# Zeroing the masked keys of three narrow-head attention blocks on GpSimd instead of masking their key-major scores on TensorE

## The chip, the cores and the metric

One core of one Trainium2 chip runs the whole program in one launch. The metric is the device time of that core in microseconds (us), the median of several runs. TensorE multiplies, VectorE (DVE in the rows) and ScalarE (ACT) work elementwise and can read PSUM, GpSimd (POOL) works elementwise on SBUF, SyncE (SP) issues loads and stores.

## What is computed

A decoder of two layers over 4 sequences of 256 tokens and width 256, all in float32. Each line is a residual step with a layer norm behind it:

```python
x = layernorm(x + L0_attn(x))            # a: 16 heads of 128, window of 64
x = layernorm(x + L0_xattn(x, ctx))      # b: 16 heads of 16, causal, first 256 rows of ctx
x = layernorm(x + L0_ffn(x))             # c: 8 experts, 2 per token
x = layernorm(x + L1_attn(x))            # d: 32 heads of 8, 8 key heads, causal
x = layernorm(x + L1_xattn(x, ctx))      # e: latent attention over 1601 keys
x = layernorm(x + L1_ffn(x))             # f: 16 heads of 16, causal; g: 8 experts, 2 per token
```

The three blocks b, d and f all compute

```python
scores = einsum('bqhd,bkhd->bhqk', q, k) * scale
scores = where(key <= query, scores, -inf)
out = einsum('bhqk,bkhd->bqhd', softmax(scores), v)
```

## The kernel before

The letters a to g name the stages, which run one after the other; `narrow_attention` (line 830) builds b, d and f. Its **unit** is four heads of one sequence; `n` counts them, 16 in b and f (`U` = 4 per sequence), 32 in d (`U` = 8). A score matrix of 256 x 256 has three blocks of 128 x 128 that matter (`TILES_OF`): two on the diagonal, numbers 0 and 2, and one under it.

The scores are computed twice. Query-major scores (a query per partition) lie in PSUM banks 0 to 2 (`A_BANK`) and serve only for the row maxima: four reductions on VectorE (`maxima`, lines 1314 to 1317). The negated maxima are transposed by TensorE (`turn_maxima`, line 1064) and added to the queries (`lower_queries`, line 1324) in spare lanes of the contraction, so that the key-major scores (a key per partition, banks 3 to 5, `B_BANK`) come out with the maximum subtracted. ScalarE takes their exponential in one instruction of 1536 columns into `PT` (`exponentials`, line 1236; the tile is called landing in b and f, d_PT in d). `values` (line 1118) multiplies `PT` with the values and with ones; VectorE inverts the sums and multiplies (`normalise`, lines 1330 and 1334).

The causal mask is a matrix product too. `mask_queries` and `mask_keys` (lines 1074, 1078) each multiply the bf16 mask by the identity into the eight diagonal blocks of a bank group, ahead of the scores that are added onto it. In the rows `mask_keys` is `ident_b,mask_b` and `mask_queries` is `mask_b,ident_b`; all of these go through the helper on line 100.

TensorE's order is written out by hand in the loop of line 1143. Iteration `i` does: `mask_queries` for unit i+2 (waits for the maxima of unit i+1), the scores of both forms (query-major for i+2, key-major for i, woven together, with `lowered` of i waited for), `turn_maxima` of i+1, `values` of i-1, a wait for the exponential of i, `mask_keys` for i+1, and then what lies beside (`beside`, line 908): projections for the next sequence, the output projection, a transposition of the next norm, in d also steps of stage e (class `Latent`). A projection in the bank `SIDE` first waits for `lowered` of i+1. VectorE does the maxima of i+2, `lower_queries` of i+1, then `normalise`, norms and additions. `PT` has two buffers: the exponential of n waits for `values` of n-2.

GpSimd has little to do in these blocks: it clears buffers, in b and f makes three tables for the router (`gate_gpsimd`, line 1480) and at the end scatters rows (`scatter`, line 1603), and in d ropes the context of stage e (`rope_context`, line 2191, four instructions for each of 4 sequences), makes its low part (`lower_kv`, line 2209, after ScalarE's `upper_kv`, line 2107) and starts on the first queries (`rope_q`, `lower_z`). `gpsimd_early` (line 2231) lists these in one run. ScalarE makes the copies of `upper_kv` in the iterations that `KEPT_BESIDE` names, and SyncE loads the context of sequences 2 and 3 when roping of sequences 0 and 1 is done (line 2032).

Of the kernel before, what the change touches and what calls it, by code (L numbers as in the profile page):

```python
# [16 lines left out]
P = 128  # L17
# [37 lines left out]
def decoder(nc, t, out):  # L55
    with ExitStack() as top:
# [773 lines left out]
        def narrow_attention(name, block, hd, heads, kv_heads, lane, before, following, carried=(3,), entering=(),  # L830
# [13 lines left out]
            with ExitStack() as sc:  # L844
# [48 lines left out]
                scored1, exped, valued = signal("scored1"), signal("exped"), signal("valued")  # L893
                inverted, o_made, summed, added = signal("inverted"), signal("o_made"), signal("summed"), signal("added")

# [76 lines left out]
                def tensor():  # L972
# [94 lines left out]
                    def masked(k):  # L1067

                        for block in (0, 2):
                            for j in range(4):  # L1070
                                at, col = place(block, j)
                                yield bank[k + at][:, col * P:(col + 1) * P], block == 0 and j < 3

                    def mask_queries():
                        for o, first in masked(A_BANK):
                            mm(o, ident_b[:], causal, first, False)
# [41 lines left out]
                    def values(n):  # L1118
# [4 lines left out]
                        pe.wait_ge(*exped.at(n + 1))  # L1123
# [19 lines left out]
                    for i in range(FIRST, LAST + 1):  # L1143
# [261 lines left out]
                def gpsimd():  # L1405
                    pool.wait_ge(*before)
# [554 lines left out]
        class Latent:  # L1961
# [3 lines left out]
            KEPT_BESIDE = {3: 0, 4: 1, 7: 2, 10: 3}  # L1965
# [225 lines left out]
            def rope_context(self, b):  # L2191
                landed, x, r, k = landings["e"], self.ctx_raw[b % 2], self.swapped[b % 2], self.roped[b % 2]
                cosines, sines = self.ropek[:, 0, :, :], self.ropek[:, 1, :, :]
                if b == 0:
# [578 lines left out]
```

## Time and profile before

| | |
|---|---|
| median of 3 runs | 2019.15 us (2017.1 to 2019.63) |
| the profiled execution | 2011.26 us, its span 2009.9 us |
| mean granted TensorE clock | 0.965 |
| TensorE, VectorE, ScalarE, GpSimd busy | 1847.1, 1291.5, 1083.5, 603.4 us |
| stage b / d / f, roughly | 290 to 420 / 598 to 830 / 1695 to 1827 us of the span |

A row of a timeline gives the start in us from the start of the span, the duration, the engine, the line of the kernel, the operation, what it writes and reads with shapes, how many instructions are merged, and in brackets how long the engine stood idle before it and what ended that. PE is TensorE's matrix product and PEld its weight load. TensorE's instructions are pipelined, so a row's duration reaches beyond the start of the next one: of two successive groups the distance of their starts tells what one costs. PEclk is the share of TensorE's full clock (2.4 GHz) that was granted; 0.50 is the low level, 1.2 GHz. The chain that ended last goes back from the last instruction, at each step to what released it.

### The profile page before, as it was taken

The page shows a single profiled execution, that of the slowest core. Times are in us where ns is not written, and L with a number is a line of the kernel's source. Part 1 is how long each engine was busy: PE and PEld are TensorE (multiplying, and loading weights), DVE is VectorE, ACT ScalarE, POOL GpSimd, SP SyncE. Part 2 cuts the span into 40 slices and gives each one's busy share as a digit, 9 for nine tenths or more (in the row PEclk, how much of TensorE's full clock was granted, in tenths as well). Part 3 has the DMA queues.
Part 4 walks back from the last instruction along what each step waited for, and adds up shares of the span by engine and source line. Part 5 has one row for each costly group of instructions (what it writes and reads, how often), then busy time and mean ns, then how long its engine had stood idle before and what let it go on. Part 6 is the DMA issues. An engine that isn't in the chain of part 4 may idle for free.

```text
span 2009.9 us, 42825 instructions
## 1 busy us (share of the span) xinstructions
PE 1847.1 (92%) x16214; PEld 1539.6 (77%) x16214; DVE 1291.5 (64%) x3373; ACT 1083.5 (54%) x2729; POOL 603.4 (30%) x543
## 2 busy tenths in 40 slices
PE   7989988979998999789999999999999997897995
PEld 6988976646656767589999999999999985774663
DVE  5576655752236555468888888888888887775222
ACT  5756653312213333468878888888888873331221
POOL 5633320032223200334444443334444430003221
PEclk9999999979998999889999999999999998997998
DMA  4000009222238000000000000000000002402223
GB/s 158 12 1 1 1 26 365 81 89 39 47 57 258 2 2 2 21 11 11 12 12 11 27 12 11 11 11 12 12 11 1 1 1 88 175 3 78 40 46 66
DMA packets 51864, 91.75 MB, mean 46 GB/s; under 512 B 4592, under 2 KB 43632, under 8 KB 49232
## 3 DMA queue, kind: packets, MB, share of 16 engines
q1 hardware_dynamic: 42784, 77.64, 11.6%
q0 software_dynamic: 8160, 10.29, 3.3%
q8 instruction: 134, 2.20, 0.4%
q10 hardware_dynamic: 720, 1.09, 0.2%
q14 instruction: 66, 0.54, 0.1%
HBM read 56.13 MB, written 32.87 MB: 44 GB/s over the span
## 4 chain that ended last, share of the span: by engine, by line
PE 72%; DVE 16%; issue 4%; ACT 3%; POOL 2%; DMA 2%; SPq 0%; ACTq 0%; DVEq 0%; POOLq 0%
PE bank L100 60%; PE bank L2355 9%; DVE e_st L2508 1%; DVE e_PT_lo L2527 1%; DVE a_t L640 1%; DVE d_nm L1315 1%; PE bank L1729 1%; POOL g_rows L1609 1%; POOL c_rows L1609 1%; PE bank L440 1%; PE bank L193 1%; DVE f_nm L1315 1%; DVE d_nm L1314 1%; DVE tiny L125 1%; DVE b_nm L1315 1%
## 5 line engine op out<-in xcount | busy, mean ns | idle before, releaser
L2508 DVE TENSOR_REDUCE e_st<-bank 128x1 f32<-128x401 f32 x512 | 291.2, 569 | 143.2 <-PE bank L100 135.7
L2445 ACT ACTIVATE e_P<-bank,e_st 128x400 f32<-128x400 f32 (+1 forms) x512 | 307.5, 601 | 104.6 <-DVE e_st L2512 103.8
L2527 DVE TENSOR_TENSOR e_PT_lo<-bank,e_PT_hi 128x512 fp32r<-128x512 f32 (+1 forms) x448 | 287.7, 642 | 0.0
L2355 PE MATMUL bank<-ident,e_P 128*128 128x128 f32 (+1 forms) x1664 | 260.4, 276 | 16.8 <-DVE e_PT_lo L2527 6.7
L2460 ACT CAST e_PT_hi<-bank 128x512 fp32r<-128x512 f32 (+1 forms) x448 | 248.3, 554 | 26.3 <-PE bank L2355 11.8
L100 PE MATMUL bank<-e_PT_hi,e_kv 128*128 128x256 f32 (+1 forms) x832 | 250.6, 321 | 0.0
L2355 PEld LDWEIGHTS bank<-ident,e_P 128*128 128x128 f32 (+1 forms) x1664 | 196.5, 141 | 53.2 <-issue 37.8
L100 PE MATMUL bank<-e_PT_lo,e_kv 128*128 128x256 f32 (+1 forms) x832 | 217.2, 281 | 0.0
L100 PE MATMUL bank<-e_KT,e_qk_hi 128*128 128x402 f32 x512 | 195.0, 381 | 9.7 <-ACT e_P L2445 6.5
L100 PE MATMUL bank<-e_KT,e_qk_lo 128*128 128x402 f32 x512 | 177.5, 347 | 0.0
L100 PEld LDWEIGHTS bank<-e_PT_lo,e_kv 128*128 128x128 f32 (+1 forms) x832 | 159.6, 192 | 0.0
L100 PEld LDWEIGHTS bank<-e_PT_hi,e_kv 128*128 128x128 f32 (+1 forms) x832 | 158.9, 191 | 0.1
L2219 POOL TENSOR_TENSOR x_in<-x_in,e_ropeq 96x512 f32<-96x512 f32 x32 | 41.2, 1287 | 343.7 <-ACT x_in L2144 343.7
L100 PE MATMUL bank<-mask_b,ident_b 128*128 128x128 bf16 (+1 forms) x878 | 123.6, 270 | 13.0 <-DVE XT_lo L206 7.1
L100 PEld LDWEIGHTS bank<-e_KT,e_qk_hi 128*128 128x128 f32 x512 | 96.4, 188 | 27.2 <-ACT e_P L2445 23.1
L2219 POOL TENSOR_TENSOR e_r<-x_in,e_ropeq 96x512 f32<-96x512 f32 x32 | 41.0, 1283 | 226.5 <-ACT x_in L2144 226.5
L100 PEld LDWEIGHTS bank<-mask_b,ident_b 128*128 128x128 bf16 x878 | 68.5, 101 | 47.9 <-issue 19.0
L2445 ACT ACTIVATION_READ_ACCUMULATOR e_P<-bank,e_st 128x1 f32 x512 | 102.6, 200 | 0.0
L100 PEld LDWEIGHTS bank<-e_KT,e_qk_lo 128*128 128x128 f32 x512 | 97.2, 190 | 0.0
L1236 ACT ACTIVATE d_PT<-bank 128x1536 f32<-128x1536 f32 x32 | 46.5, 1452 | 89.0 <-PE bank L100 89.0
L1236 ACT ACTIVATE landing<-bank 128x1536 f32<-128x1536 f32 x32 | 46.4, 1451 | 81.9 <-PE bank L100 81.9
L100 PE MATMUL bank<-g_wall,g_xT 128*128 x184 | 88.0, 602 | 0.8 <-ACT g_xT L1783 0.8
(448 smaller groups left out, 4935.8 us busy)
## 6 DMA issues: line engine op xcount, KB each, us to landing
c_wall<-in_c_w SPq DMA_DIRECT2D x8, 1536.0 KB, 19.2
g_wall<-in_g_w SPq DMA_DIRECT2D x8, 1536.0 KB, 19.5
c_rows<-normed SPq DMA_DIRECT2D x9, 1040.0 KB, 12.0
g_rows<-normed SPq DMA_DIRECT2D x9, 1040.0 KB, 12.9
e_stage<-in_e_w SPq DMA_DIRECT2D x16, 416.0 KB, 3.2
c_xs<-c_rows SPq DMA_DIRECT2D x23, 130.0 KB, 2.1
g_xs<-g_rows SPq DMA_DIRECT2D x23, 130.0 KB, 2.1
landing<-in_a_wo SPq DMA_DIRECT2D x2, 1024.0 KB, 6.1
```

Source lines behind the costliest of these rows:

```text
L100: return pe.matmul(o, a, b, start=start, stop=stop, skip_group_check=True)
L125: dve.tensor_tensor(s, s, v, ALU.mult).then_inc(link.sem, 1)
L193: last = pe.transpose(view[:, c, i * P:(i + 1) * P], src[:, i, c * P:(c + 1) * P], ident[:])
L1236: act.activation(PT[n % 2].rearrange("p a j n -> p (a j n)"), psum[:, B_BANK:B_BANK + 3, :].rearrange("p a n -> p (a n)"), ACT.Exp, scale= ...
L1315: dve.tensor_reduce(out1[:, 0:3], a[:, :, P:3 * P], AX.X, ALU.max, negate=True)
L1609: pool.indirect_dma_start(scratch[self.name][0][:, :], bass.IndirectOffsetOnAxis(ap=self.slots[:, n, k:k + 1], axis=0), self.payload[:, n, ...
L2219: pool.tensor_tensor(x1, v, self.ropeq[:, 0:2, :], ALU.mult)
L2355: last = pe.transpose(o[0:rows, c * SEQ + i * P:c * SEQ + (i + 1) * P], p[:, i, k0:k0 + rows], ident[:])
L2445: act.activation(Pm[u % 2][:, i, j * PIECE:j * PIECE + n], bank[score_bank[j]][:, 0:n], ACT.Exp, bias=s[:, i, 4:5], accum_out=s[:, i, j:j ...
L2460: act.copy(PT[at % PT_BUFS][0][0:rows, 0:n, :], bank[tb_bank[at % 2]][0:rows, 0:n * SEQ].rearrange("p (c n) -> p c n", c=n)).then_inc(*pt_ ...
L2508: last = dve.tensor_reduce(s[:, i, j:j + 1], bank[score_bank[j]][:, 0:PIECE + 1], AX.X, ALU.max)
L2527: dve.tensor_tensor(lo, bank[tb_bank[at % 2]][0:rows, 0:n * SEQ].rearrange("p (c n) -> p c n", c=n), hi.bitcast(F32), ALU.subtract).then_i ...
```

## The change

`mask_keys` goes. The key-major scores are computed without the mask; the first product into each of their three banks (head j = 3) now carries the start flag, and the wait for the exponential of the unit before (or, for the first unit, for `v_kept`) stands in `scores` instead of ahead of `mask_keys`. GpSimd then zeroes the exponentials of keys behind their query: `select(n)` waits for the exponential of n and runs two `affine_select` in place on `PT`, over six and two blocks of 128 x 128, and `values(n)` waits for `selected` instead of `exped`. `mask_queries` stays.

Since `select(n)` is wanted in each unit, GpSimd's other work is spread: the router's tables come after the select of unit 1, and in d `rope_context` is cut into three parts that follow the selects of units 0 to 11, with `lower_kv` after those of units 3, 4, 8 and 12. ScalarE's `upper_kv` of sequences 2 and 3 moves from iterations 7 and 10 to 8 and 12.

```diff
-                    def mask_keys():
-                        for o, first in masked(B_BANK):
-                            mm(o, causal, ident_b[:], first, False)
...
-                        return mm(o, k if keys_first else q, q if keys_first else k, False, True)
+                        return mm(o, k if keys_first else q, q if keys_first else k, keys_first and j == 3, True)
...
                         if n1 is not None:
                             pe.wait_ge(*lowered.at(n1 + 1))
+                            if n1 == 0:
+                                pe.wait_ge(*v_kept.at(1))
+                            else:
+                                pe.wait_ge(*exped.at(n1))
...
-                        pe.wait_ge(*exped.at(n + 1))
+                        pe.wait_ge(*selected.at(n + 1))
...
-                        if 0 <= i + 1 < N:
-                            if i >= 0:
-                                pe.wait_ge(*exped.at(i + 1))
-                            else:
-                                pe.wait_ge(*v_kept.at(1))
-                            mask_keys()
...
+                    def select(n):
+
+                        p = PT[n % 2]
+                        pool.wait_ge(*exped.at(n + 1))
+                        for blocks, pattern in ((p[:, :, 0:3:2, :], [[0, 3], [0, 2], [1, P]]), (p[:, 0:3:2, 3, :], [[0, 2], [1, P]])):
+                            last = pool.affine_select(blocks, blocks, pattern=pattern, compare_op=ALU.is_ge, fill=0.0, base=0,
+                                                      channel_multiplier=-1)
+                        last.then_inc(*selected.up())
+
...
+                    if ahead:
+                        ahead.gpsimd_first()
+                    for i in range(N):
+                        select(i)
+                        if routing and i == 1:
+                            routing.gate_gpsimd()
+                        if ahead:
+                            ahead.gpsimd_beside(i)
                     if routing:
-                        routing.gate_gpsimd()
                         routing.scatter(0)
                     if ahead:
-                        ahead.gpsimd_early()
+                        ahead.gpsimd_last()
...
-            KEPT_BESIDE = {3: 0, 4: 1, 7: 2, 10: 3}
+            KEPT_BESIDE = {3: 0, 4: 1, 8: 2, 12: 3}
...
+            ROPED_BESIDE = {0: (1, 0), 1: (1, 1), 2: (1, 2), 5: (2, 0), 6: (2, 1), 7: (2, 2), 9: (3, 0), 10: (3, 1), 11: (3, 2)}
+            LOWERED_BESIDE = {3: 0, 4: 1, 8: 2, 12: 3}
+
+            def gpsimd_first(self):
+                for part in range(3):
+                    self.rope_context(0, part)
+
+            def gpsimd_beside(self, i):
+                if i in self.ROPED_BESIDE:
+                    self.rope_context(*self.ROPED_BESIDE[i])
+                if i in self.LOWERED_BESIDE:
+                    self.lower_kv(self.LOWERED_BESIDE[i])
+
+            def gpsimd_last(self):
                 self.rope_q(0)
                 self.lower_z(0)
```

## Rows read from the trace of the kernel before

**Rows 1.** page, part 1: engine, busy us (share), instructions

```profile
PE 1847.1 (92%) x16214; PEld 1539.6 (77%) x16214; DVE 1291.5 (64%) x3373; ACT 1083.5 (54%) x2729; POOL 603.4 (30%) x543
```

**Rows 2.** chain that ended last, 344 to 354 us: start, us, engine, output, line

```profile
347.48 0.34 DVE b_q L1324
347.86 2.12 PE bank L100 x36
```

**Rows 3.** timeline of the same unit: start, us, engine, line, op, output<-inputs, count

```profile
347.06 0.41 DVE L1317 TENSOR_REDUCE b_nm<-bank 128x1 f32<-128x256 f32 x1
347.17 0.45 PEld L100 LDWEIGHTS bank<-ident_b,mask_b 128*128 128x128 bf16 x8 [0.20 <-ACT landing L1236]
347.17 0.62 PE L100 MATMUL bank<-ident_b,mask_b 128*128 128x128 bf16 x8
347.40 0.41 DVE L1324 TENSOR_TENSOR b_q<-b_q,bank 128x256 f32<-128x256 f32 x1
347.86 0.39 PE L100 MATMUL bank<-b_wv_hi,b_ctx 128*128 128x256 f32 x1
```

**Rows 4.** timeline of a unit without a projection, block f

```profile
1791.80 1.45 ACT L1236 ACTIVATE landing<-bank 128x1536 f32<-128x1536 f32 x1 [5.33 <-PE bank L100]
1793.38 0.41 DVE L1317 TENSOR_REDUCE f_nm<-bank 128x1 f32<-128x256 f32 x1
1793.48 0.62 PE L100 MATMUL bank<-ident_b,mask_b 128*128 128x128 bf16 x8
1793.94 0.61 PE L100 MATMUL bank<-mask_b,ident_b 128*128 128x128 bf16 x8
1796.77 0.86 PE L100 MATMUL bank<-landing,f_V 128*32 128x256 f32 x16
```

**Rows 5.** timeline of two units where TensorE never waits, blocks b and d

```profile
402.70 0.62 PE L100 MATMUL bank<-ident_b,mask_b 128*128 128x128 bf16 x8
403.16 1.51 PE L100 MATMUL bank<-b_wo,x_in 128*128 128x256 f32 x6
...
814.90 0.89 PE L100 MATMUL bank<-ident_b,mask_b 128*128 128x128 bf16 x8
815.62 0.61 PE L193 MATMUL bank<-ident,X 128*128 128x128 f32 x4
```

**Rows 6.** timeline of GpSimd alone: its three kinds of elementwise work

```profile
291.02 2.69 POOL L1408 MEMSET b_V<- 128x1536 f32 x2 [14.88 <-DVE X L665]
323.03 0.29 POOL L1486 CAST c_earlier<-landing 128x128 bf16<-128x128 f32 x1
...
645.76 1.95 POOL L2211 TENSOR_TENSOR e_kv<-e_roped,e_kv 128x832 fp32r<-128x832 f32 x1 [26.88 <-ACT e_kv L2109]
```

**Rows 7.** chain that ended last at the ends of blocks b and f

```profile
407.02 1.46 ACT landing L1236
408.53 4.28 PE bank L100 x56
...
1813.15 1.46 ACT landing L1236
1814.65 4.28 PE bank L100 x56
```

**Rows 8.** timeline at the end of block d

```profile
818.15 1.45 ACT L1236 ACTIVATE d_PT<-bank 128x1536 f32<-128x1536 f32 x1 [1.29 <-PE bank L100]
821.04 0.86 PE L100 MATMUL bank<-d_PT,d_V 128*32 128x256 f32 x16
```

**Rows 9.** stretches of block b: us, busy by engine, PEclk granted, DMA share, GB/s

```profile
396.00:399.00 3.00, 2.07 (x23) 1.71 (x26) 1.84 (x5) 0.59 (x1) 0.00 (x0) 1.00 0.00 0
399.00:403.00 4.00, 4.00 (x52) 2.26 (x47) 0.57 (x2) 1.45 (x1) 0.00 (x0) 0.57 0.01 4
```

**Rows 10.** timeline of TensorE after its two long waits in block b

```profile
311.59 0.38 PE L100 MATMUL bank<-XT_hi,b_wq_hi 128*128 128x256 f32 x1 [1.55 <-DVE b_q L1324]
...
396.87 0.66 PE L193 MATMUL bank<-ident,X 128*128 128x128 f32 x4 [1.14 <-DVE b_nm L1317]
```

More of the change, by code:

```diff
@@ L1065, in turn_maxima, with mask_queries @@
                         last.then_inc(*nm_turned.up())
-                    def masked(k):
+                    def mask_queries():
                         for block in (0, 2):
@@ L1071, in masked @@
                                 at, col = place(block, j)
[L1072 to L1076, printed above, removed]
-                    def mask_keys():
-                        for o, first in masked(B_BANK):
-                            mm(o, causal, ident_b[:], first, False)
+                                mm(bank[A_BANK + at][:, col * P:(col + 1) * P], ident_b[:], causal, block == 0 and j < 3, False)
                     def score(n, block, j, keys_first):
@@ L2188, in vector, with rope_context @@
                     self.lower_r(0, o)
-            def rope_context(self, b):
+            def rope_context(self, b, part):
                 landed, x, r, k = landings["e"], self.ctx_raw[b % 2], self.swapped[b % 2], self.roped[b % 2]
                 cosines, sines = self.ropek[:, 0, :, :], self.ropek[:, 1, :, :]
-                if b == 0:
-                    pool.wait_ge(*landed[0].at(16))
-                    pool.wait_ge(*landed[1].at(16))
-                elif b == 1:
-                    pool.wait_ge(*landed[2].at(16))
-                else:
-                    pool.wait_ge(*self.ctx_in[b - 2].at(16))
-                    pool.wait_ge(*self.x_roped.at(b - 1))
-                    pool.wait_ge(*self.kv_lo.at(b - 1))
-                pool.tensor_tensor(r[:, :, 0:32], x[:, :, 32:64], sines[:, :, 0:32], ALU.mult)
-                pool.tensor_tensor(r[:, :, 32:64], x[:, :, 0:32], sines[:, :, 32:64], ALU.mult)
-                pool.tensor_tensor(k[:], x, cosines, ALU.mult).then_inc(self.twice.sem, 1)
-                pool.wait_ge(self.twice.sem, self.twice.step())
-                pool.tensor_tensor(k[:], k[:], r, ALU.add).then_inc(*self.x_roped.up())
+                if part == 0:
+                    if b == 0:
+                        pool.wait_ge(*landed[0].at(16))
+                        pool.wait_ge(*landed[1].at(16))
+                    elif b == 1:
+                        pool.wait_ge(*landed[2].at(16))
+                    else:
+                        pool.wait_ge(*self.ctx_in[b - 2].at(16))
+                        pool.wait_ge(*self.x_roped.at(b - 1))
+                        pool.wait_ge(*self.kv_lo.at(b - 1))
+                    pool.tensor_tensor(r[:, :, 0:32], x[:, :, 32:64], sines[:, :, 0:32], ALU.mult)
+                    pool.tensor_tensor(r[:, :, 32:64], x[:, :, 0:32], sines[:, :, 32:64], ALU.mult)
+                elif part == 1:
+                    pool.tensor_tensor(k[:], x, cosines, ALU.mult).then_inc(self.twice.sem, 1)
+                    self.twice.step()
+                else:
+                    pool.wait_ge(self.twice.sem, self.twice.value)
+                    pool.tensor_tensor(k[:], k[:], r, ALU.add).then_inc(*self.x_roped.up())
             def lower_kv(self, b):
@@ L2229, in lower_z @@
                 pool.tensor_tensor(lo[:], self.r1[m % 2], hi[:].bitcast(F32), ALU.subtract).then_inc(*self.z_lo.up())
-            def gpsimd_early(self):
-                self.rope_context(0)
-                self.rope_context(1)
-                for b in range(BATCH):
-                    self.lower_kv(b)
-                    if b + 2 < BATCH:
-                        self.rope_context(b + 2)
+            ROPED_BESIDE = {0: (1, 0), 1: (1, 1), 2: (1, 2), 5: (2, 0), 6: (2, 1), 7: (2, 2), 9: (3, 0), 10: (3, 1), 11: (3, 2)}
[9 more added lines that the diff above has]
+            def gpsimd_last(self):
                 self.rope_q(0)
```

2 lines of the change are left out of this document (1 added, 1 removed).

## The prediction, made before the changed kernel was run

> **What bounds the kernel now.** I read the page's part 1 first: TensorE has an instruction in flight for 92% of the span [rows 1], so the 512 mask products that go look like a straight saving on the busiest engine. They are eight of 128 columns per unit (four heads of one batch element; 16, 32 and 16 units in blocks b, d and f), and a group of eight takes 0.46 us from its start to the next instruction's [rows 4, 5]. If all 64 groups were on the path, 64 x 0.46 = 29.4 us would go. So the next view is the chain that ended last, in the middle of a block: there it doesn't run through TensorE from end to end. In each unit it leaves TensorE after the scores, goes through the four row maxima on VectorE and the addition of the negated maxima to the queries (line 1324), and comes back to TensorE only when that addition is done [rows 2]. The timeline of that unit shows where the mask group lies. It starts at 347.17 and is through 0.46 us later, at 347.63; the addition ends at 347.81 and the projection behind it starts at 347.86 [rows 3]. The group fills a wait for VectorE.
>
> **The mask products.** I went through the 64 groups in the timelines of the three blocks and looked at what ends just before the next TensorE instruction. In 45 of them it is VectorE, 0.05 us before, as in rows 3: the removal leaves TensorE idle for 0.46 us more and changes no time. Nor does the wait for the exponential gain anything there; it stood ahead of the group and now stands ahead of the scores, later still. In 12 units without a projection, or with the entering transposition next, the query mask or a transposition follows, which needs only the last maximum. That ends at 1793.79 and could release TensorE at 1793.83 instead of 1793.94 [rows 4]: 0.1 us each, 1.2 us in all. In 7 units TensorE is late itself and nearly the whole group counts: 0.46 us for the one at 402.70, 0.72 for the one at 814.90 that ran partly on the low clock [rows 5]; with the other five between 0.3 and 0.46 this is 3.0 us. **Gain: 4.2 us**.
>
> **What `affine_select` costs.** Block by block GpSimd now makes two in-place instructions per unit, 768 and 256 elements per partition, 1024 in all. No row shows this operation. Below stands the memset, which reads nothing: 2.69 us for two of 1536 elements, so 0.88 ns an element and 0.90 us for 1024. Above stands the subtraction with two inputs: 1.95 us for 832, so 2.34 ns an element and 2.4 us [rows 6]. The cast has one input, as the select has, but at 128 elements in 0.29 us its fixed part and its rate can't be told apart; 2.3 ns an element is its upper reading [rows 6]. Between 0.9 and 2.4 I take 1.7 us, the middle, because the select has one input but an index and a comparison beside it, and call the whole step, with 0.1 us for the extra hop to and from GpSimd, S = 1.8 us.
>
> The Trainium skill (GPSIMD Engine Reference, section 3.1) gives about 1.8 cycles an element at 1.2 GHz for a tight loop; by it the two would take some 1.5 us, an estimate, and the sum below would be about 0.6 us lower. No row here can show it.
>
> **Where S lies beside other work.** The products with the values wait for the select instead of the exponential. In a unit in the middle they run one unit later: the exponential of rows 4 ends at 1793.25 and its values start at 1796.77, 3.5 us later, and this is among the shortest units. S fits in with 1.7 us to spare, so it costs nothing there. If the cover were gone (S above 3.5 us) every microsecond more would fall on the path once in two units, since the values hold back the scores two units on.
>
> **Where S is exposed.** At the end of a block no scores follow. In b the exponential ends at 408.48 and the values start at 408.53, in f at 1814.61 and 1814.65, and the chain of both blocks runs through them [rows 7]; the norms, the router's products and the scatter on GpSimd are queued behind. S goes on the path in full: 2 x 1.8 = 3.6 us. In d there are two pieces of other work in between: the exponential ends at 819.60, the values start at 821.04 [rows 8]. Of S 1.44 us is covered, and 0.4 is left. **Cost: 4.0 us**.
>
> **The moved steps.** GpSimd in block d also ropes the context (four instructions per batch element) and makes the low parts of it. These go from one run ahead of the units into slots between the selects, one of at most 2.1 us per unit. Behind a select of 1.8 us this is 3.9 us in a unit of 5.4 or more, so the next select finds the queue empty; TensorE needs their result only several units later, and the copies on ScalarE that feed them (line 2109) shift by one and two units in the same direction. The first roping stays ahead of the first select, but its inputs have landed and it is over long before the first exponential. In b and f the gate's tables go behind the second select and are needed only at the end. The loads on SP's queue wait for roping of the first two batch elements, one of which ends some units later; its slot is five units ahead of the use. I cost all of these at nothing; what hides them is the same VectorE cycle as above. The flags that start the accumulation in PSUM change no duration.
>
> **The clock.** This is the cost I can't fix. TensorE's granted clock goes to its low level for stretches: at 396 to 399 us it is 1.00 with TensorE busy 2.07 of 3 us, and in the next 4 us 0.57, so 3.4 us at 1.2 GHz instead of 2.4 [rows 9]. What went before is a wait of 1.14 us. But after a wait of 1.55 us in the same block it stayed up [rows 10]. A fall costs at most 1.7 us, about 1 when part of the slower work is under VectorE. The removed groups leave a wait of 0.20 (for the exponential, ahead of the group) + 0.69 (347.17 to 347.86) = 0.9 us [rows 3] in each of the 45 units like that of rows 3, and at the ends of b and f a new one of 1.9 us. I count two extra falls, at the block ends, 2 us.
>
> **Sum.** The profiled execution took 2011.3 us. 2011.3 - 4.2 + 4.0 + 2.0 = 2013.1. The median of the runs is 2019.15, 7.9 above the profiled one, so the forecast is 2019.15 + 1.8, rounded to **2021.0 us**. About 0.2%, 4 us, is what a measurement of this kernel can tell from no change.
>
> **The rivals.**
> *The low clock comes often (slower).* The mechanism is that of the last paragraph but one, in the middle of the blocks: a wait of 0.9 us in each unit of 5.5 is close to the 1.14 us after which it fell. For it: the stretches [rows 9]. Against: the clock stayed up after the wait of 1.55 us [rows 10]. It decides from three further falls on. One in six of the 45 units would be 7 or 8 falls, at 1 us each with the block ends 2029 us. The Trainium skill (TensorE: Matmul & The Clock Gate, HAM oscillation) describes such falls after repeated waits; whether waits this short suffice, only the run can show.
> *The mask products were on the path after all (faster).* If the wait for VectorE were shorter than the trace says, because the release of line 1324 comes with TensorE's own delay, up to 29 us would go; half of the 45 units would give about 2009. For it: in 12 units the ends of VectorE's last maximum and of the mask group are only 0.1 us apart [rows 4]. Against: the 0.05 us between VectorE's end and TensorE's start, the same in 45 units.
> *The select is slow (slower).* At 5 us it would overrun the cover by 1.5 us in every second unit: 32 x 1.5 = 48, plus 3 x 3.2 at the block ends, some 2079 us. Against: no elementwise row of GpSimd is above 2.4 ns an element.
> The Trainium skill (GPSIMD Engine Reference, section 3.1) puts data-dependent branching at 12 cycles an element, by which, an estimate, the select would take about 10 us and GpSimd would bound the blocks.
> *The change doesn't do what it says* would be a select without cover because GpSimd's other work delays it in d; that costs 1 or 2 us in some of the units and lies within the range.
>
> **How the numbers follow.** Forecast 0.55, with its own range 2015 to 2026 (S between 1.1 and 2.7 moves the sum from -2 to +3, none to four falls). Of it 0.05 is faster, 0.42 the same, 0.08 slower. Low clock often 0.26, slower. Mask products on the path 0.12, faster. Slow select 0.07, slower. Together: faster 0.17, same 0.42, slower 0.41. The range takes in the forecast's, most of the low-clock case and the near end of the faster one: 2012 to 2035.
>
> **What would show it.** In the timeline of a unit as in rows 3 the projection should start 0.05 us after line 1324 as before, with a wait of 0.9 us ahead of it, and the unit should stay at 5.5 us. The select should take 0.9 to 2.4 us and end before the values' turn. At the ends of b and f the chain should show GpSimd between ScalarE and TensorE. PEclk in the stretches of the blocks tells the clock rival; a unit that is shorter by 0.46 tells the second; values waiting for GpSimd in the middle of a block the third. The forecast is wrong if the select differs from 1.7 us by more than 1.5, or if the number of falls changes by more than four.

## The result and the profile after

| | before | changed |
|---|---|---|
| median, 12 runs each | 2017.16 us (2010.62 to 2020.75) | 2024.87 us (2020.88 to 2030.12) |
| ratio, 95% interval | | 1.0036 (1.0027 to 1.0046) |
| the profiled execution | 2011.26 us, span 2009.9 | 2030.12 us, span 2028.9 |
| mean granted TensorE clock in it | 0.965 | 0.956 |

The change costs 7 us: slower by 0.36%, where 0.2% is what can be told from no change. The profiled execution of before lies near the low end of its kernel's spread and that of the changed kernel is the longest of its twelve, so their difference, 19 us, isn't the change's. One execution of a later run (mask_back_again) took 4497 us and is left out of all its figures. The lengths of the stages show where it is (each from its first matrix product to the next one's, in us; in brackets the time on the low clock, as twice the sum of 1 - PEclk over stretches of 1 us). The third line is the changed kernel once more, on another chip:

```
              a          b          gate to wall  c        d          e          f           gate to wall  g
before        297.7(14)  112.3(7)   36.6(21)  153.3(3)  231.8(24)  863.8(24)  120.6(7)   36.2(20)  155.7(18)
changed       299.2(20)  116.2(17)  39.9(21)  153.0(3)  236.0(34)  862.5(17)  125.0(17)  39.5(28)  155.7(18)
changed again 299.3(17)  113.5(10)  35.8(20)  152.0(0)  235.4(27)  863.7(24)  125.1(17)  35.6(17)  156.6(19)
```

The first pieces of the feed-forward stages (gate to wall, from the router's first product to the first with the experts' weights) are 40 and 39.5 us long in the changed kernel and 36 in its second execution. Another kernel that was run on two chips (mask_back, below) has 36.0 on one and 40.3 on the other for the first of them, and of eleven profiles of the experiments below the four on the first chip have 35.6 to 36.2 us for either piece, the seven on that second chip and a third 38.5 to 40.3. That difference goes with the chip. What belongs to the change is in d, about 4 us, in f, 4.5, and in b, 1 to 4, and the low clock is longer in all three.

Page, part 1, of the changed kernel, answers to [rows 1]:

```profile
PE 1826.5 (90%) x15702; PEld 1519.7 (75%) x15702; DVE 1298.5 (64%) x3373; ACT 1083.7 (53%) x2729; POOL 682.1 (34%) x671
```

The 512 products are gone, TensorE is busy 20.6 us less, GpSimd 78.7 us more in 128 new instructions. VectorE has the same 3373 instructions and is busy 7.0 us longer, though nothing in the change touches it. So VectorE is where to look first.

The middle of a block is as it was. The chain at the place of [rows 2]; the numbers are start and us:

```profile
346.59 0.34 DVE b_q L1315
...
346.97 2.12 PE bank L100 x36
```

And the timeline there, with the exponentials of two successive units, their selects (L1402) and the first products with the values:

```profile
346.11 1.23 POOL L1402 TENSOR_SCALAR_AFFINE_SELECT landing<-landing 128x768 f32<-128x768 f32 x2 [5.25 <-ACT landing L1227]
346.18 0.41 DVE L1308 TENSOR_REDUCE b_nm<-bank 128x1 f32<-128x256 f32 x1
346.51 0.41 DVE L1315 TENSOR_TENSOR b_q<-b_q,bank 128x256 f32<-128x256 f32 x1
346.97 0.39 PE L100 MATMUL bank<-b_ctx,b_wk_hi 128*128 128x256 f32 x1 [0.62 <-DVE b_q L1315]
350.14 1.45 ACT L1227 ACTIVATE landing<-bank 128x1536 f32<-128x1536 f32 x1 [0.94 <-PE bank L100]
351.66 1.23 POOL L1402 TENSOR_SCALAR_AFFINE_SELECT landing<-landing 128x768 f32<-128x768 f32 x2 [4.32 <-ACT landing L1227]
...
355.68 1.45 ACT L1227 ACTIVATE landing<-bank 128x1536 f32<-128x1536 f32 x1 [1.75 <-PE bank L100]
355.93 0.86 PE L100 MATMUL bank<-landing,b_V 128*32 128x256 f32 x16
```

Line 1315 is line 1324 of before. The projection starts 0.05 us after it ends, as in [rows 3], now behind a wait: 0.62 us by its own row, 0.89 by the row of its weight load. The unit takes 5.54 us (350.14 to 355.68) as before. Both parts of the select take 1.23 us, from 351.66 to 352.89, and the values come at 355.93, 3 us later.

At the ends of b and f the chain has the select in it, where [rows 7] had nothing between ScalarE and TensorE:

```profile
411.19 1.46 ACT landing L1227
...
412.71 1.25 POOL landing L1402 x2
...
414.01 4.28 PE bank L100 x56
...
1827.61 1.46 ACT landing L1227
...
1829.12 1.24 POOL landing L1402 x2
```

From the end of the exponential to the values it is 1.36 us where it was 0.05. At the end of d, in the timeline:

```profile
830.73 1.45 ACT L1227 ACTIVATE d_PT<-bank 128x1536 f32<-128x1536 f32 x1 [1.29 <-PE bank L100]
832.25 1.23 POOL L1402 TENSOR_SCALAR_AFFINE_SELECT d_PT<-d_PT 128x768 f32<-128x768 f32 x2 [3.02 <-ACT d_PT L1227]
833.63 0.86 PE L100 MATMUL bank<-d_PT,d_V 128*32 128x256 f32 x16
```

The values start 1.45 us after the exponential (832.18), and it was 1.44 [rows 8]: the select fits in whole.

**Where VectorE's 7 us are.** Its groups by line, the one that grew most, first before and then after (busy us, mean ns of one):

```profile
L125 DVE TENSOR_TENSOR tiny<-tiny 128x2 f32<-128x2 f32 x84 | 19.4, 232 | 2.9
```

```profile
L125 DVE TENSOR_TENSOR tiny<-tiny 128x2 f32<-128x2 f32 x84 | 22.4, 266 | 2.9
```

Lines 123, 125, 127, 142, 145 and 155 are the small steps of the layer norm, on two elements per partition; together they grew by 6.7 us. The chain through one norm in d shows how. Before:

```profile
696.88 0.67 DVE tiny L132 x2
...
698.26 0.18 DVE tiny L145
...
698.46 0.17 DVE tiny L123
...
698.66 0.17 DVE tiny L125
...
699.01 0.47 DVE d_nm L1314
```

After, the same norm:

```profile
706.84 0.67 DVE tiny L132 x2
...
708.23 0.73 DVE tiny L145
...
708.98 0.32 DVE tiny L123
...
709.32 1.89 DVE tiny L125
...
711.40 0.47 DVE d_nm L1305
...
713.64 5.00 PE bank L100 x44
```

And GpSimd beside it, in the timeline:

```profile
708.03 1.25 POOL L1402 TENSOR_SCALAR_AFFINE_SELECT d_PT<-d_PT 128x768 f32<-128x768 f32 x2 [3.33 <-ACT d_PT L1227]
709.26 1.93 POOL L2222 TENSOR_TENSOR e_kv<-e_roped,e_kv 128x832 fp32r<-128x832 f32 x1
```

The norm takes 4.56 us (706.84 to 711.40) instead of 2.13. Three of its instructions end when an instruction of GpSimd does: line 145 at 708.96, when the larger part of the select, which takes 0.87 us, is over, line 123 at 709.30 with the select's end (709.28), line 125 at 711.21 with the end of line 2222 (711.19). The norm stands on the chain, ahead of the row maxima, and TensorE waits behind them. The stretches of these places, first before and then after (us, busy by engine, PEclk):

```profile
697.00:701.00 4.00, 2.36 (x42) 1.47 (x42) 3.76 (x15) 1.00 (x1) 0.00 (x0) 1.00 0.02 4
701.00:705.00 4.00, 3.66 (x64) 3.32 (x68) 3.76 (x11) 2.02 (x4) 0.00 (x0) 1.00 0.00 0
```

```profile
708.00:711.00 3.00, 0.77 (x22) 0.33 (x12) 2.88 (x4) 0.73 (x1) 2.97 (x3) 1.00 0.00 0
711.00:714.00 3.00, 0.36 (x1) 0.36 (x2) 2.96 (x8) 0.00 (x0) 0.19 (x1) 0.52 0.00 0
714.00:718.00 4.00, 4.00 (x32) 3.71 (x35) 3.29 (x10) 1.39 (x3) 0.00 (x0) 0.50 0.00 0
```

From 708 to 714, while the norm is held up and the row maxima follow it, TensorE is busy 1.1 us of 6; it has the low clock from 711 until 718. From one exponential to the next this unit (the 13th distance in d) takes 13.19 us, and 9.11 before.

### The profile page after: what moved, and what is told of

Its sections match the earlier page's. It is cut to its first block, busy times and chain, and to the rows that moved or that the text cites. A ratio compares the mean times of both kernels' runs of the same rounds, so it can differ in the third digit from the quotient of the medians.

```text
span 2028.9 us, 41994 instructions
## 1 busy us (share of the span) xinstructions
PE 1826.5 (90%) x15702; PEld 1519.7 (75%) x15702; DVE 1298.5 (64%) x3373; ACT 1083.7 (53%) x2729; POOL 682.1 (34%) x671
## 3 DMA queue, kind: packets, MB, share of 16 engines
q8 instruction: 130, 2.13, 0.4%
## 4 chain that ended last, share of the span: by engine, by line
PE 71%; DVE 17%; issue 4%; ACT 3%; POOL 3%; DMA 2%; SPq 0%; ACTq 0%; DVEq 0%; POOLq 0%
PE bank L100 59%; PE bank L2374 9%; DVE d_nm L1306 1%; DVE e_st L2527 1%; DVE e_PT_lo L2546 1%; DVE a_t L640 1%; PE bank L1736 1%; DVE d_nm L1305 1%; POOL c_rows L1616 1%; POOL g_rows L1616 1%; PE bank L440 1%; DVE tiny L125 1%; PE bank L193 1%; DVE f_nm L1306 1%; DVE b_nm L1306 1%
## 5 line engine op out<-in xcount | busy, mean ns | idle before, releaser
L1402 POOL TENSOR_SCALAR_AFFINE_SELECT landing<-landing 128x768 f32<-128x768 f32 x64 | 39.4, 640 | 198.6 <-ACT landing L1227 198.6
## 6 DMA issues: line engine op xcount, KB each, us to landing
g_rows<-normed SPq DMA_DIRECT2D x9, 1040.0 KB, 13.2
```

Source lines behind the costliest of these rows:

```text
L1402: last = pool.affine_select(blocks, blocks, pattern=pattern, compare_op=ALU.is_ge, fill=0.0, base=0, channel_multiplier=-1)
```

## The experiments

Two theories stood after this. **Contention**: GpSimd's new instructions hold up the norms on VectorE, and the norms are on the path; 2.5 us more are the selects at two block ends. **The clock**: without the mask products TensorE has longer pauses and runs more often on the low clock. A rival to both is that each select costs a little in every unit, by its hop or through the values that start later. All experiments were timed in five rounds beside the kernel before on the same chip. "Low clock" is the mean over all timed runs of 2 x (1 - granted clock) x span, minus that of the kernel before.

| kernel | ratio (95%) | low clock, us |
|---|---|---|
| after_again | 1.0050 (1.0031 to 1.0069) | +23 |
| mask_back | 1.0044 (1.0029 to 1.0060) | -2 |
| mask_back_again | 1.0045 (1.0028 to 1.0062) | -4 |
| no_mask_no_select | 1.0009 (0.9995 to 1.0022) | +17 |
| paced_only | 1.0009 (0.9994 to 1.0025) | 0 |
| kv_moved | 1.0053 (1.0040 to 1.0066) | +22 |
| kv_moved_roped_first | 1.0055 (1.0042 to 1.0068) | +26 |
| last_unit_masked | 1.0045 (1.0032 to 1.0058) | +21 |
| first_and_last_masked | 1.0009 (1.0000 to 1.0018) | +2 |
| select_off_norms | 1.0001 (0.9991 to 1.0011) | -2 |
| select_at_norms | 1.0036 (1.0023 to 1.0049) | -7 |
| masks_back_at_norms | 0.9998 (0.9985 to 1.0010) | 0 |

### The two halves of the change

`mask_back` is the changed kernel with `mask_keys` restored: everything of the select, none of the removal.

```diff
+                        if 0 <= i + 1 < N:
+                            ...
+                            mask_keys()
```

> The changed kernel with the eight mask products per unit put back on TensorE, in their old place; the select on GpSimd and the order of GpSimd's work stay as changed. The result is the same as before's, masked twice. Theory GpSimd (the selects and the moved steps hold up VectorE's small norm instructions, and S = 1.2 us stands at the block ends): 5 to 9 us slower than before, VectorE busy about 1298 us as in the changed kernel against 1291.5, the stretched instructions of 0.7 to 1.9 us still there. Theory clock (waits of 0.9 us on TensorE, left by the mask products, bring the low clock): about 3 us slower than before, only the block ends, and the time on the low clock in blocks b, d and f as before (7, 24 and 7 us).

`no_mask_no_select` is the kernel before without `mask_keys` and without a select. The mask of the key-major scores is left out of the computation, and the exponentials are scaled down.

```diff
-                            mask_keys()
...
-                                       scale=scale)
+                                       scale=scale / 64)
```

> The kernel before with the eight mask products per unit taken out of the key-major scores and nothing in their place: GpSimd's work as before, no select. The keys behind their query are left unmasked, and the exponentials' scale is divided by 64 so that they stay finite, so the attention of b, d and f is not the reference's. Theory clock: same as before or slower by up to 5 us, with the time on the low clock in b, d and f up by some 10 us in each as in the changed kernel. Theory GpSimd: 3 to 4 us faster than before (the 4.2 us of the prediction), low-clock time unchanged, VectorE busy 1291 us.

`paced_only` is the kernel before with the order of GpSimd and ScalarE of the change: the roping between the units, each step behind a wait for the exponential.

```diff
-                        ahead.gpsimd_early()
+                        ahead.gpsimd_first()
+                    for i in range(N):
+                        pool.wait_ge(*exped.at(i + 1))
...
+                            ahead.gpsimd_beside(i)
```

> The kernel before with only the order of GpSimd's other work changed: roping in three parts and the low parts after the exponentials of the same units as in the changed kernel, the router's tables after unit 1, ScalarE's copies in units 8 and 12; no select, mask products kept. Theory GpSimd: block d longer by 2 to 4 us, with VectorE's L125 near the norm of the first sequence stretched to the length of the subtraction on GpSimd, 1.9 us; in all 2 to 4 us slower. Theory clock: same as before within 1 us.

> The changed kernel again, on the chip of the other three. 5 to 9 us slower than before. Where the profile of a second execution differs from the first by more than some us (low clock, the waits of VectorE for something outside the core at the starts of c and g), that part of the 19 us between the two profiled spans is the execution's and not the change's.

The two halves add up: 1.0044 with the select alone, 1.0009 with the removal alone, 1.0050 with both. The select half loses 8.5 us and has no more low clock than before. The removal half has 17 us more low clock and gains nothing (between 1 us faster and 4 slower): the clock's case of that expectation came, not the other, which was 3 to 4 us faster. The order of GpSimd alone is at 1.0009, which can't be told from nothing; I had expected 2 to 4 us, and a long line 125, which isn't there. Another step of a norm is: line 163, which scales X, in the timeline of paced_only, beside the roping that the new order has put there.

```profile
620.09 2.41 DVE L163 TENSOR_SCALAR X<-X,tiny 128x256 f32<-128x256 f32 x2
...
620.41 1.94 POOL L2214 TENSOR_TENSOR e_roped<-landing 128x832 f32<-128x832 f32 x1 [2.55 <-ACT d_PT L1236]
```

Line 163 runs twice here, once for each half of the rows, and the two take 0.73 us elsewhere in it; the second was held until just after the roping step ended. So the moved steps alone already hold up a norm, by 1.7 us.

So most of the loss is in the select, but the one thing that I knew it to cost, the ends of b and f, is 2.6 us of 8.5.

### Taking single causes away

`kv_moved` takes line 2222 out of the norm shown above, and leaves the select there:

```diff
-            KEPT_BESIDE = {3: 0, 4: 1, 8: 2, 12: 3}
+            KEPT_BESIDE = {3: 0, 4: 1, 8: 2, 14: 3}
...
-            LOWERED_BESIDE = {3: 0, 4: 1, 8: 2, 12: 3}
+            LOWERED_BESIDE = {3: 0, 4: 1, 8: 2, 14: 3}
```

> The changed kernel with one step of block d moved: ScalarE's copy and GpSimd's low part for the last sequence come with unit 14 instead of 12. Theory port (a VectorE instruction on the norm's small tiles stands still until the GpSimd instruction beside it is through): the 1.88 us instruction of line 125 goes back to 0.16 us, unit 13 of block d from 13.2 to 13.7 us down to 9.1 to 10, the kernel 3 to 4 us faster than the changed one, so 5 to 8 us slower than before instead of 8 to 12. Rival (the two selects ahead of the scores hold unit 13): no change, unit 13 at 13 us.

`kv_moved_roped_first` also ropes the second sequence ahead of the units instead of beside the first three.

```diff
-            ROPED_BESIDE = {0: (1, 0), 1: (1, 1), 2: (1, 2), 5: (2, 0), 6: (2, 1), 7: (2, 2), 9: (3, 0), 10: (3, 1), 11: (3, 2)}
+            ROPED_BESIDE = {5: (2, 0), 6: (2, 1), 7: (2, 2), 9: (3, 0), 10: (3, 1), 11: (3, 2)}
```

> As kv_moved, and the second sequence is roped ahead of the first unit's select as before the change, not beside units 0 to 2 of block d. Theory port: the stretched VectorE instructions of 0.5 to 2.4 us at the start of block d (lines 127, 142, 155, 163) are gone, units 1 to 4 of block d together 29 to 30 us instead of 30 to 34, another 1 to 2 us faster than kv_moved. Rival (roping ahead delays the first select): the first values wait for GpSimd, no gain or 1 us slower.

Both expectations were missed in time: 1.0053 and 1.0055, no better than the changed kernel. The chain of kv_moved through that norm shows that the edit did its work:

```profile
702.69 0.73 DVE tiny L145
...
703.44 0.32 DVE tiny L123
...
703.79 0.17 DVE tiny L125
...
706.38 4.61 PE bank L100 x44
```

Line 125 is at 0.17 us again, where it had 1.89; what the select does is still there. The unit takes 11.06 us (12.18 in kv_moved_roped_first, whose code is the same there and which spends 6.8 instead of 3.4 us of the unit on the low clock), and 13.2 to 13.7, with 6.8 us of low clock in each, in the six executions with line 2222 and the select beside the norm. It doesn't get back to 9.11. So line 2222 is worth 1 to 2.7 us, 0.1% of the time, and that is less than what five rounds tell; the rest of the profile of kv_moved has more low clock elsewhere, 31 us of it in stage e (24 before), which isn't touched. In kv_moved_roped_first the stretched steps at the start of d are gone, as expected, but its first four distances add up to 31.0 us, not to 29 or 30, with 15 us of low clock in them. Taking a stretched step away didn't take its low clock away, and what brings that in a given execution isn't shown.

`last_unit_masked` masks the last unit of each block on TensorE and has no select there.

```diff
-                        select(i)
+                        if i < N - 1:
+                            select(i)
```

> The changed kernel with the last unit of each block masked by TensorE as before, without a select. Theory tail: the values of the last unit start 0.05 us after the exponential again instead of 1.4 us after it; 1.4 us at the ends of b and f, up to 0.4 of it given back for the mask group, so 2 us faster than the changed kernel. Rival (the end of a block waits for the norm on VectorE anyway): no change.

`first_and_last_masked` is kv_moved_roped_first with units 0, 1 and the last of each block masked on TensorE.

```diff
+                ON_PE = (0, 1, N - 1)
...
+                        if i + 1 in ON_PE:
+                            ...
+                            mask_keys()
```

> All of it together: kv_moved_roped_first, the last unit masked on TensorE, and the first two units of each block as well, where TensorE would wait longest. Theory port and clock: b, d and f spend as little time on the low clock as before (7, 24 and 7 us), their first units take 5.5 and 6.5 us again instead of 7.0 and 7.9 to 9.2, and of the masks' gain 1 to 3 us are left: 0 to 4 us faster than before. If the low clock comes from the middle units: slower than before by 3 us or more.

Without the select at the ends the values start 0.05 us after the exponential again, and the ratio is 1.0045, against 1.0053 for kv_moved on the same chip; 2 us are possible, but the intervals overlap. With units 0 and 1 masked on TensorE as well, most of the loss is gone (1.0009) and so is nearly all of the extra low clock (+2 us instead of +26), though it isn't faster than before, where I had expected 0 to 4 us. The profiles show where the clock differs. TensorE's waits for the lowered queries in unit 1 of b, in the timeline before and after, with the mask group between them before:

```profile
317.20 0.62 PE L100 MATMUL bank<-ident_b,mask_b 128*128 128x128 bf16 x8 [1.19 <-ACT landing L1236]
318.07 0.39 PE L100 MATMUL bank<-b_ctx,b_wk_hi 128*128 128x256 f32 x1 [0.25 <-DVE b_q L1324]
```

```profile
321.97 0.56 PE L100 MATMUL bank<-b_ctx,b_wk_hi 128*128 128x256 f32 x1 [2.06 <-DVE b_q L1315]
```

And the stretches after these starts, again before and after:

```profile
318.00:320.00 2.00, 1.93 (x36) 1.74 (x36) 1.76 (x11) 1.15 (x2) 0.00 (x0) 1.00 1.02 436
```

```profile
322.00:324.00 2.00, 2.00 (x16) 1.71 (x16) 1.76 (x10) 0.79 (x2) 0.35 (x1) 0.51 0.99 424
```

The two waits of 1.19 and 0.25 us have become one of 2.06, the clock is at its low level behind it, and the unit takes 7.11 us instead of 5.54 (the next one 6.77 instead of 7.50). In the first unit of f it is the same, 7.91 (and 9.20 in after_again) for 6.48. Of all fourteen profiles, six have no mask product in unit 1 (the changed one, after_again, no_mask_no_select, kv_moved, kv_moved_roped_first, last_unit_masked). In five of them the clock fell in unit 1 of b and of f. In kv_moved_roped_first it stayed at 1.00 behind the same wait of 2.06 us. With the mask product it fell in none of eight. So the falls in unit 1 are rarer with the product; what decides one in a single execution stays open.

The removal doesn't only add falls. In the last two distances of f there is low clock in six of the eight profiles without mask products in the middle units, and in none of the six with them. In b it is the other way round: at least 3.4 us in all six with them, and none in six of the eight without. So a fall in unit 1 of b is partly paid back at the block's end: from first to last exponential, b takes 89.9 us in no_mask_no_select and 91.3 before, and f takes 101.5 and 98.3.

### Only the norms, and all but the norms

Here the masks are on TensorE everywhere, as in mask_back, so the selects can be left out one by one. I listed the units of mask_back whose select, or the GpSimd step behind it, overlapped a small step of a norm: 0, 1, 12 and 20 in d, 0, 1, 3 and 5 in f, and the last units.

```diff
+                NORMS = {"b": (15,), "d": (0, 1, 12, 20, 31), "f": (0, 1, 3, 5, 15)}[name]
+                SELECT = [n for n in range(N) if n not in NORMS]
...
-                        select(i)
+                        if i in SELECT:
+                            select(i)
+                        else:
+                            pool.wait_ge(*exped.at(i + 1))
```

The list has eleven units: the eight above and three last ones. The expectations below say ten, one too few; 53 selects are left in select_off_norms, not 54.

> As mask_back (masks still on TensorE, selects on GpSimd beside them), but without the select in ten of its 64 units: those whose select or the step behind it ran beside a layer norm on VectorE in the profile of mask_back (d: 0, 1, 12, 20, f: 0, 1, 3, 5), and the last of each block. The masks are in place anyway, so nothing of the computation is left out. Contention theory (the norm's 128x2 instructions stretch beside GpSimd, the norm is on the path, plus 1.2 us at each end): most of mask_back's 8.5 us goes, 1 to 3 us over the kernel before are left, about paced_only's 1.2; no 128x2 instruction of VectorE above 0.4 us in d's units 13 and 21; unit 13 of d at 9.1 to 10.4 us. Rival (each select costs a little in every unit, by the hop and the later start of the values): 54 of 64 selects are left, so some 7 us over the kernel before.

`select_at_norms` has `n in NORMS` in that list.

> The complement: as mask_back, but with the select in those ten units alone. Contention theory: 6 to 9 us over the kernel before, unit 13 of d at 13 us, and all of mask_back's stretched 128x2 instructions are there again. Rival (a small cost in each unit): 10 of 64 selects and two block ends, 3 us over the kernel before at most.

> mask_back once more, on the chip of select_off_norms and select_at_norms, so that the three can be compared: 6 to 9 us over the kernel before, as the first time, with no more time at the low clock than before has. Both theories expect the same.

This settles the rival. 53 selects cost nothing that can be measured (1.0001, between 2 us faster and 2 slower), and the other eleven cost what all 64 cost (1.0036 against 1.0045, intervals overlapping). The pair alone doesn't tell a norm from the start or the end of a block, since three of the eleven are last units and four are the first two of d and f; unit 12 of d, in the middle of its block, does. The chain through the same norm, first select_off_norms, then select_at_norms:

```profile
705.05 0.18 DVE tiny L145
...
705.25 0.17 DVE tiny L123
...
705.45 0.17 DVE tiny L125
```

```profile
708.24 0.73 DVE tiny L145
...
708.99 0.33 DVE tiny L123
...
709.34 1.89 DVE tiny L125
```

Of the 7 us of those eleven units, some 2.8 us are the ends of b and f, where the values start 1.45 and 1.44 us after the exponential instead of 0.05. The rest is in d: its 31 distances between exponentials sum to 208.2 us in select_at_norms and to 201.2 in select_off_norms, with 3.2 us in the 13th (13.63 and 10.38) and 2.1 in the 2nd (14.38 and 12.32). These are single executions, with 20.5 and 13.7 us of low clock in d, so the 7.0 us are more than d's share. In f each of the four norms has one step stretched by 0.2 us, and no distance is longer but one with a fall of the clock.

### The change without its two costs

The changed kernel with those eleven units, and units 0 and 1 of b, given back to TensorE:

```diff
+                ON_PE = {"b": (0, 1, 15), "d": (0, 1, 12, 20, 31), "f": (0, 1, 3, 5, 15)}[name]
```

> The changed kernel, with the ten units of select_at_norms and unit 1 of b given back to TensorE: their masks are products again and have no select; the other 53 units have the select and no mask product. GpSimd's and ScalarE's order is that of the change. Contention theory with the clock: the select costs nothing now (select_off_norms: 1.0001), and what is left is what taking mask products away costs in units at which the clock does not fall: -3 to +2 us against before. If wider waits in the middle units bring the low clock by themselves: +3 us or more, and the granted clock lower than before's. Rival (moving the masks to GpSimd costs a little in each unit): +5 us or more.

0.9998 (0.9985 to 1.0010), and no more low clock than before. 51 of 64 units have no mask product for their keys and a select on GpSimd, and no cost or gain can be measured. With unit 0 of b, which is in the list too, thirteen units are masked on TensorE; the 53 of the expectation should read 51. In its profile the clock falls once in b after the first exponential, in the second distance, which leads to unit 2, the first without the product (8.94 us instead of 7.50). GpSimd and VectorE aren't always apart here; this is the timeline beside the same norm's end:

```profile
696.51 1.94 POOL L2239 TENSOR_TENSOR e_kv<-e_roped,e_kv 128x832 fp32r<-128x832 f32 x1 [4.17 <-ACT e_kv L2133]
```

It runs beside the row maxima (696.62 to 698.48), and in the chain these take 0.47, 0.87, 0.20 and 0.33 us, as they do when GpSimd is idle. The maxima read PSUM; the norm's small steps work on SBUF alone. No kernel was faster than the one before.

## Why the prediction was half right

The time is inside the range and 4 us above the number forecast; the ratio says slower, where the likeliest case was no measurable change. The forecast stood on a median of three runs, 2019.15 us, which twelve runs put at 2017.16. As a change it was +1.8 us and +7.7 were measured, so 2 us of a miss of 6 are hidden by that, by luck. By its steps:

**What bounds the kernel, and the 45 hidden groups: right.** The units in the middle of the blocks have the length that they had, and the projection still starts 0.05 us behind VectorE. The removal of 512 products from the busiest engine gained nothing that could be measured (1.0009 in no_mask_no_select, 0.9998 in masks_back_at_norms). The 12 units with 0.1 us each came out so where they can be compared: 4.64 instead of 4.72 us for the 3rd, 12th and 13th distance in b. The late units give less than the 0.46 us that I took for a whole group: 0.27 in the 6th, 14th and 22nd distance of d, 0.41 in the last distance of each block. Over the 56 of 61 distances that have an execution without low clock on both sides the removal gains about 2.6 us in all, where I had 4.2. The rival with the products on the path has fallen. (Its number was off too: half of the 45 units at 0.46 us is 10 us, so 2011, not 2009.)

**The select's duration: over-sized.** 1.23 us plus 0.1 for the hops, where I took 1.8; it is 1.2 ns an element, nearer to the memset (0.88) than to the subtraction (2.34). The cost at the block ends was 1.3 + 1.3 + 0 instead of 1.8 + 1.8 + 0.4, so 2.6 us instead of 4.0. The slow select has fallen with it. The Trainium skill (GPSIMD Engine Reference, section 3.1) would have had 1.5 us by its rate for a tight loop, an estimate, nearer than my 1.7 and still above the 1.23 of the trace.

**Where the select lies beside other work: right as far as it went, and too short.** I asked only whether the values would wait for it. They don't. 53 selects cost nothing that can be measured. But I followed the new instruction's result, and not what runs on the other engines while it works.

**The moved steps at nothing, and GpSimd's instructions at nothing for the others: wrong, and the main miss.** "What hides them is the same VectorE cycle as above": that cycle was the thing they disturbed. GpSimd was free for most of the blocks before and is now busy 1.3 to 3.4 us in each unit. Where that falls on a layer norm, the norm waits, and the norm is in the cycle. mask_back against before puts the select half at 8.5 us, of which 2.6 are the ends. That it is the meeting with the norms, and not the select as such, is shown by the pair select_off_norms and select_at_norms with the chain in unit 12 of d. The profile of before had the material: the norm on the chain in d, GpSimd idle beside it, and the hold-up itself. In stage a of before, eleven of the norms' small steps take 1.15 to 1.22 us, each until an instruction of GpSimd is through, as here:

```profile
108.69 1.19 DVE L145 TENSOR_SCALAR tiny<-tiny 128x2 int32<-128x2 int32 x1
```

```profile
108.58 1.28 POOL L740 TENSOR_TENSOR a_qT_lo<-a_t,a_qT_hi 128x512 fp32r<-128x512 f32 x1 [2.21 <-ACT a_qT_hi L537]
```

The Trainium skill has the rule (SBUF — State Buffer, Who interferes with whom): an instruction of VectorE with two inputs in SBUF and one of GpSimd that reads SBUF share a port pair, and the later one is blocked until the first is through. The trace agrees, with line 125, which has two inputs in SBUF, ending 0.02 us after line 2222, and with the maxima, from PSUM, not slowed. The rule as told here is for two inputs; lines 142, 145 and 155 have one and were held up too (line 145: 0.73 us for 0.18).

**The clock: right in kind, too small, and at another place.** I counted two more falls, at the block ends, 2 us. A select at the end brought none there: up to the first product with the experts' weights mask_back has 20.5 and 17.1 us of low clock behind b and f, and paced_only, without a select and on the same chip, 20.5 and 20.5. Over all runs the removal alone brings 17 us more on the low clock. In the profiles it lies at the starts of b and f and in f's last two distances. The first distance grows by 1.4 to 2.7 us by it, and there the mask group stood in the middle of a pause of 2 us. My own list of waits stopped at the 45 like [rows 3] and the ends; the 7 in which TensorE is late and the first units weren't looked at for what the group does to the clock. What the falls cost in all wasn't measured by itself. With a gain of 2.6 us and no_mask_no_select at +2 it would be some 4.6; 17 us at 1.1 to 1.5 us for each 3.4 (below) would be 5.5 to 7.5. Within the interval of 5 us of that run the two agree.

**The rival of a low clock in the middle units: fallen.** With 51 units without the product, most of them open to the wait of 0.9 us, the time on the low clock is the same as before (masks_back_at_norms, 0 us). The Trainium skill (TensorE: Matmul & The Clock Gate, HAM oscillation) tells of falls after repeated waits; waits of this length didn't bring them here.

**The sum.** By the runs it is +2 for the removal (2.6 us of gain against a cost of the clock of about 4.6, which is only the difference) and +8.5 for the select half, 2.6 of them the block ends and 6 the norms with what follows them on TensorE: +10.5, where after_again measured +10 us against the kernel before and the first pair of 12 runs +7.7. I had -4.2 + 4.0 + 2.0. The term that was missing is the largest.

What stays open: how much the new order costs by itself. In paced_only the first distance of d is 4.64 us against 6.24 before and the second, with the long line 163, 12.23 against 7.36; the first four together are 2.3 us longer, but the ratios (1.0009, and 1.0001 for select_off_norms, which has the same order and the same long line) can't tell it from nothing. Whether the falls in unit 1 come in a given execution is open too. And the parts of the +6 for the norms, the waiting and the clock after it, were not separated by a run.

## What to carry to other kernels

When work goes to an engine that was idle, look at what the others do in the same stretch and where their operands lie, as well as at who waits for its result: a busy-time total of an engine that the change doesn't touch, before and after, finds this in one line. Products that fill a pause of TensorE cost nothing here and may be worth something, since with them the clock fell in unit 1 in none of eight profiles and without them in five of six; before such products are removed, list the pauses in which one stands. That is a count of executions, and why it is so isn't shown. And select_off_norms with select_at_norms is a cheap form of test: with the old way restored everywhere, the new one can be switched on unit by unit.

## What the runs showed of the hardware

- Instructions of VectorE on 128x2 elements in SBUF, which take 0.16 to 0.18 us, took 0.31, 0.72 and 1.88 us beside GpSimd, each until an instruction of GpSimd was through; between two instructions of GpSimd just one got in. Larger ones are held up as well: two of 128x256 (line 163) took 2.41 us instead of 0.73. The row maxima, which read PSUM, took as long beside GpSimd as without it.
- In unit 12 of d a hold-up of 2.4 us in a norm was followed by up to 6.8 us of low clock on TensorE, and the unit grew by 4.1 us (9.11 to 13.19).
- `affine_select` on 1024 float32 elements per partition took 1.23 us in two instructions, in place.
- One spell of low clock made a unit 1.1 to 1.5 us longer: 11.06 and 12.18 us for the same unit in kv_moved and kv_moved_roped_first, 7.36 and 8.82 in the tenth of b, 6.48 and 7.91 in the first of f.
